# The membrane scan of a spiking mixer: three chains over thirds of the chunks in place of one chain per batch

## What is computed

```python
def step(carry, inputs):
    ...
    inp_t = r_t * wkv
    reset = spike_fn(mem - THRESH)
    mem = BETA * mem + inp_t - reset * THRESH
    spk = spike_fn(mem - THRESH)
    return ((sa, sb, mem), spk)
```

## Time and profile before

| | |
|---|---|
| Time, median of 3 runs | 629.06 us (627.97 to 631.52) |
| The profiled execution, whole | 630.46 us |
| Its span, first to last instruction | 628.6 us |
| Busy: PE, DVE, ACT, POOL | 81%, 72%, 55%, 49% of the span |
| Granted PE clock, mean | 0.916 of full speed |
| Instructions of the scan | 256 on DVE, 51.22 to 96.4 us |

### The profile page before, as it was taken

The page is one execution under the profiler, slowest core; times in us unless marked ns, Lnnn a source line. Parts: engine busy times, 40 slices in busy tenths (PEclk is TensorE's granted clock), DMA queues, the critical chain, the costliest instruction groups (busy, mean ns, idle before and its releaser), DMA issues. The chain is left out here.

```text
span 628.6 us, 11742 instructions
## 1 busy us (share of the span) xinstructions
PE 506.1 (81%) x3926; PEld 313.4 (50%) x3926; DVE 454.5 (72%) x1201; ACT 348.9 (55%) x992; POOL 308.4 (49%) x248
## 2 busy tenths in 40 slices
PE   3740004679999999799879999999799887999996
PEld 3310002337677766544336777676444333666774
DVE  4899997688888883645688888883545675257775
ACT  3950000569998996634469999995633332632331
POOL 5660001488888888447578888883100254020000
PEclk9975556699999999899989999999999988799998
DMA  8200000201111112000011111111000000000001
GB/s 296 103 0 1 0 0 2 68 17 44 36 35 36 35 35 83 3 1 1 19 54 38 37 35 35 35 41 31 0 1 1 1 0 0 2 0 1 18 19 33
DMA packets 14048, 18.80 MB, mean 30 GB/s; under 512 B 2171, under 2 KB 8613, under 8 KB 13861
## 3 DMA queue, kind: packets, MB, share of 16 engines
q1 hardware_dynamic: 13700, 17.97, 10.4%
q10 hardware_dynamic: 288, 0.08, 0.1%
HBM read 8.87 MB, written 1.05 MB: 16 GB/s over the span
## 5 line engine op out<-in xcount | busy, mean ns | idle before, releaser
L465 ACT ACTIVATE prob<-psS,nmx 128x128 f32<-128x128 f32 x256 | 89.9, 377 | 22.1 <-DVE nmx L1007 22.1
L583 POOL TENSOR_TENSOR rst<-mv,half 128x4 f32<-128x4 f32 x24 | 24.9, 1036 | 153.0 <-DVE mv L802 137.5
L722 POOL TENSOR_TENSOR rn<-ssq,half 128x16 f32<-128x16 f32 x32 | 93.2, 2913 | 7.0 <-DVE ssq L993 6.6
L714 POOL TENSOR_TENSOR ra<-ra,rb 128x512 f32<-128x512 f32 x64 | 80.2, 1275 | 2.9 <-DVE rb L975 2.9
L352 ACT ACTIVATE lnx<-psT,nmr,rst 128x128 f32<-128x128 f32 x52 | 19.5, 458 | 91.2 <-POOL nmr L584 91.2
L1284 PE MATMUL psQK<-wqkv,hsA 128*128 128x512 f32 x128 | 64.6, 630 | 3.3 <-ACT z L358 2.2
L972 DVE TENSOR_TENSOR ra<-psQK,rope 128x512 f32<-128x512 f32 x64 | 43.9, 685 | 20.4 <-PE psQK L1284 20.3
L1007 DVE TENSOR_REDUCE nmx<-psS 128x4 f32<-128x512 f32 x64 | 41.2, 685 | 21.3 <-PE psS L1363 18.3
L465 ACT ACTIVATION_READ_ACCUMULATOR prob<-psS,nmx 128x1 f32 x256 | 55.5, 217 | 0.0
L730 POOL TENSOR_TENSOR qkn<-ra,rn 128x512 f32<-128x512 f32 x32 | 33.4, 1043 | 35.7 <-DVE qkn L1001 35.7
L1290 PE MATMUL psO<-masks,identb 128*128 128x512 bf16 x12 | 5.3, 630 | 54.8 <-DVE vAB L878 54.8
(11 more groups left out here) (225 smaller groups left out, 1196.5 us busy)
## 6 DMA issues: line engine op xcount, KB each, us to landing
vAB<-vAB SPq DMA_DIRECT2D x62, 128.0 KB, 2.2
wqkv<-in_wqkv SPq DMA_DIRECT2D x2, 768.0 KB, 7.9
big<-in_x SPq DMA_DIRECT2D x4, 256.0 KB, 4.3
ropeb<-in_rope SPq DMA_DIRECT2D x1, 1024.0 KB, 7.3
big<-in_ew SPq DMA_DIRECT2D x2, 512.0 KB, 4.2
out<-big SPq DMA_DIRECT2D x4, 256.0 KB, 2.3
wmod<-in_wmod SPq DMA_DIRECT2D x1, 768.0 KB, 6.4
w<-in_w SPq DMA_DIRECT2D x2, 341.0 KB
```

The source lines that it names most:

```text
L465: act.activation(prob[:, k, :], psS[:, hb, c * P:(c + 1) * P], ACT.Exp, bias=nmx[:, k:k + 1], accum_out=sums[:, n % 2, k:k + 1]).then_inc( ...
L714: pool.tensor_tensor(o, o, rb[:, r], ALU.add).then_inc(s["sum_" + name], 1)
L722: pool.tensor_tensor(rn[:, :], ssq[:, :], half[:, :], ALU.pow).then_inc(s["rn_ready"], 1)
```

## The change

The chunks' range is cut into three parts, 21, 21 and 22 chunks, and a chain takes one such part of both batches: 42, 42 and 44 elements per instruction. A third semaphore, `dve_c`, is added. A step is then six instructions on DVE, three times L874 and three times L878. vst is cleared for two of the three chains by a memset each. The first three passes are written out in a Python loop in place of the device's loop, and the fallback has three chains as well. What a chunk starts from is unchanged: its predecessor's end of the pass before. PE's wait for `dve_b` has the same value and means the same place in the passes.

```diff
--- before.py
+++ after.py
@@ -182,7 +182,7 @@
             ln_t1 ln_var ln_rstd ln_norm ln_t2 ln_out
             xT_fill xT_evac
             kv_mm num_ready ek_ready gek_ready ekv_ready sb_ready den_ready r_mm r_ready rcp_ready quot_ready cur_ready x_mixed
-            dve dve_b act_own pool_own fallback fallback_b rope_ready tabs_phase tabs_ready z_ready hsA_ready
+            dve dve_b dve_c act_own pool_own fallback fallback_b fallback_c rope_ready tabs_phase tabs_ready z_ready hsA_ready
             k_mm q_mm sq_k sq_q ssq_k ssq_q rope_k rope_q sum_k sum_q ssq_max rn_ready q_ready k_ready
             v_fill v_evac qT_fill qT_evac kT_fill kT_evac pT_fill pT_evac oT_fill oT_evac
             s_done negmax p_ready pv_done va_up0 va_up1 va_low0 va_low1 o_norm
@@ -864,19 +864,22 @@
                 return ph[:, :, j:j + SEQ * (NCH - 1) + 1:SEQ]
 
 
-            both = [own, Steps(dve, s["dve_b"])]
-            both[1].did(dve.memset(vst[:, 1, :], 0.0))
+            thirds = [slice(k * NCH // 3, (k + 1) * NCH // 3) for k in range(3)]
+            chains = [own, Steps(dve, s["dve_b"]), Steps(dve, s["dve_c"])]
+            for k in range(1, 3):
+                chains[k].did(dve.memset(vst[:, :, thirds[k]], 0.0))
 
             def membrane_pass(steps):
                 for j in range(SEQ):
-                    for b in range(B):
-                        steps[b].sync()
-                        steps[b].did(dve.scalar_tensor_tensor(out=vst[:, b, :], in0=at(j)[:, b, :], scalar=-0.3,
-                                                              in1=cur[:, b, :, j], op0=ALU.mult, op1=ALU.add))
-                    for b in range(B):
-                        steps[b].sync()
-                        steps[b].did(dve.scalar_tensor_tensor(out=at(j + 1)[:, b, :], in0=at(j)[:, b, :], scalar=-1.0,
-                                                              in1=vst[:, b, :], op0=ALU.is_lt, op1=ALU.subtract))
+                    for k in range(3):
+                        steps[k].sync()
+                        steps[k].did(dve.scalar_tensor_tensor(out=vst[:, :, thirds[k]], in0=at(j)[:, :, thirds[k]], scalar=-0.3,
+                                                              in1=cur[:, :, thirds[k], j], op0=ALU.mult, op1=ALU.add))
+                    for k in range(3):
+                        steps[k].sync()
+                        steps[k].did(dve.scalar_tensor_tensor(out=at(j + 1)[:, :, thirds[k]], in0=at(j)[:, :, thirds[k]],
+                                                              scalar=-1.0, in1=vst[:, :, thirds[k]], op0=ALU.is_lt,
+                                                              op1=ALU.subtract))
 
 
             dve.wait_ge(s["rcp_ready"], NG)
@@ -885,12 +888,9 @@
             dve.wait_ge(s["r_ready"], NG)
             own.one(dve.tensor_tensor(ekv[:, c], ekv[:, c], rsg[:, c], ALU.mult))
             dve.wait_ge(s["cur_ready"], NG - 1)
-            with dve.Fori(0, PASSES - 1) as k:
-                for st in both:
-                    st.enter(k, 2 * SEQ)
-                membrane_pass(both)
-            for st in both:
-                st.leave(PASSES - 1)
+            for _ in range(PASSES - 1):
+                membrane_pass(chains)
+            for st in chains:
                 st.sync()
 
             def checked_pass(steps):
@@ -911,13 +911,13 @@
                 one(dve.tensor_copy(cnti[0:1, 0:1], cntf[0:1, 4:5]))
                 return dve.value_load(cnti[0:1, 0:1], min_val=0, max_val=P * B * NCH)
 
-            changed = checked_pass(both)
+            changed = checked_pass(chains)
             with dve.If(changed != 0):
 
 
-                again = [Steps(dve, s["fallback"]), Steps(dve, s["fallback_b"])]
-                for b in range(B):
-                    again[b].did(dve.memset(vst[:, b, :], 0.0))
+                again = [Steps(dve, s["fallback"]), Steps(dve, s["fallback_b"]), Steps(dve, s["fallback_c"])]
+                for k in range(3):
+                    again[k].did(dve.memset(vst[:, :, thirds[k]], 0.0))
                 changed = checked_pass(again)
                 with dve.If(changed != 0):
                     with dve.Fori(0, NCH) as k:
```

## The result

| | before | after |
|---|---|---|
| Time, median | 628.51 us (4 runs, 627.79 to 631.52) | 638.18 us (4 runs, 635.77 to 641.28) |
| Ratio | | 1.0123 (95%: 1.0088 to 1.0157) |
| Ratio, measured a second time | | 1.0100 (1.0075 to 1.0124) |
| Span of the profiled execution | 628.6 us | 634.6 us |
| Scan, first L874 to L904 | 45.3 us | 52.6 us |

By these ratios the change makes the kernel 1.0 to 1.2% slower, 6.3 to 7.7 us. They are not the quotients of the medians, which lie further apart: 9.7 us here and 7.3 us (638.01 against 630.75) the second time. The four executions of the kernel after differ by 5.5 us among themselves, so the firmest figure for the change is the length of the scan in the trace, +7.3 us. The forecast was +6.5 us with 635.6 us in all, and a range of 632.3 to 641.3. In the changed kernel L876 and L880 are what L874 and L878 were.

What follows compares the result with a forecast made beforehand. The prediction took the membrane scan, uncovered by other engines and running at DVE's own pace, as the bound. +7.1 - 0.76 + 0.15 = +6.5 us on 629.06 gave 635.6 us, range 632.3 to 641.3.

Steps and rivals of the forecast that it cites:

- What sets the pace: Membrane scan: DVE's own pace, 171 ns per instruction, sets it; two chains leave 52 ns slack per phase, no stall to fill.
- Length less 83 ns: Scan on DVE: each instruction starts about 83 ns before its predecessor ends, so pace is its length less 83 ns.
- Step (a): Scan: three instructions per phase instead of two, 397 ns against 341 over 128 phases, +7.1 us; bounds +4.6 and +13.4.
- Step (b): Scan's device loop removed: entry 0.19 us and two pass turns of 0.31 and 0.26 us saved, -0.76 us.
- Step (c): One more memset, and one more wait in the two places where all chains are collected; +0.15 us.
- Step (e): DVE's jump over the skipped fallback after the count: taken as 0, with -3.8 to +3.8 us kept for the range.
- Step (d): PE after the scan: pause before transposes grows from 4.6 to about 5.1 us; clock shift taken as 0, 1.7 us either side.
- The stride's cost as a start-up price: Rival on the scan: the stride's extra cost is fixed per instruction and doesn't shrink with elements; 641.9 us, chance 0.15.
- The waiting chains: Rival on the scan: chains wait for their own previous results, so a third chain makes it faster; 623.3 us, chance 0.04.
- the wash: Rival on the scan: pace purely proportional to elements, so a phase stays 341 ns; 628.4 us, chance 0.07.
- The pace of contiguous rows: Rival on the scan: stride costs nothing, 66 ns at 6 elements plus 1.04 per further element; 624.7 us, chance 0.03.

Runs made afterwards that it cites:

- experiment 4: Kernel before with one chain of all 128 elements instead of two of 64, passes written out; 636.43 us against 630.34, ratio 1.0102.
- two_written: Kernel before with its two chains of 64 kept and only the first three passes written out; 626.11 us against 630.34, ratio 0.993.
- experiment 8: The kernel after measured and profiled once more, unedited; 638.01 us against 630.75 for the kernel before, ratio 1.0100.
- experiment 3: Kernel before with each of its two chains taking half the chunks of both batches, as two rows of 32; 630.92 us against 630.34, ratio 1.0011.
- experiments 5: As the kernel after, but with four chains of 32 elements and a fallback with one chain; 643.27 us in a single execution.
- experiment 7: Against the kernel before: states and currents stored contiguously, passes written out, one-chain fallback; two chains 620.13 us against 629.98, three chains 627.33 us.
- before_near: Kernel before with only the skipped fallback shortened to one chain; 628.77 us against 630.75, ratio 0.9950.

## Why the prediction was right

- *What sets the pace.* Right. Two chains run at DVE's own pace; experiment 4 shows the other state and gives the dependence 34 ns after the end, as the earlier trace rows had it. The argument that decided it, the second instruction of a phase that waits for nothing in that phase, holds.
- *"Length less 83 ns".* As a rule it was wrong, and that it led to nearly the right number is partly luck. Between two executions the same instructions last 253 or 276 ns (before, two_written) at the same 171 ns from start to start, so in two_written the rule would have been "length less 105"; two executions of the kernel after have 220 and 212 ns (experiment 8). The pace belongs to the instruction, the length reported for it also holds something that varies. It would have been sounder to forecast the pace from paces: 171 at 64 elements and 66 at 6 give 1.81 per element, and with it the same 132 ns at 42.7.
- *Step (a), +7.1 us.* The mis-sized term. The pace at 42.7 elements is 134.8 ns, not 132.3, and the slope is 1.70, not 1.8. The rows taken for it were of other operations (L823 with 4 elements, L904 a two-operand comparison); that this is the reason isn't shown. Measured +8.1 us, 52.6 against the 44.5 of two_written. Both bounds, +4.6 and +13.4, held it. The rows of 21 cost nothing, as taken (experiment 3).
- *Step (b), -0.76 us.* In the scan it is -0.78 (two_written) and -0.68 with three chains, but this agreement is partly luck. The forecast counted 0.19 us for the entry. The entry gives back 0.09: the first instruction comes 0.14 us after its releaser with the passes written out, not 0.04, and it lies ahead of the scan as measured. In its place stands the hole of 0.18 us in pass 1, which the prediction put at nothing when it read pass 4 alone. Together the loop's end brings about -0.87 us.
- *Step (c), +0.15 us.* L900 comes 0.13 us after its last result where it was 0.10, L904 likewise: +0.06. The two memsets together take the 0.07 us that one took.
- *Step (e), 0.* The jump is the same, 3.82 us idle in both. That its price can change with the target's place was right, with 2.25 us, not 3.8; it just didn't happen between these two kernels. In two_written it did, and in a forecast for that one the same step would have missed half of the gain.
- *Step (d).* PE's pause before L936's result is 5.7 us, forecast 5.1. From PE's start to L904 it is 0.66 us longer (101.0 to 104.34, before 93.8 to 96.51), and the 12 warming matmuls took 0.42 us less (4.86 for 5.28), which the step didn't have. Executions of one kernel differ by 3 to 4 us beside a different clock, about the whole width of the 1.7 us allowed to each side. The second measurement shows no lasting share of it in the change.
- *The sum.* +6.5 forecast, +7.3 in the scan of the trace (+8.1 for (a), -0.8 for (b)), 6.3 and 7.7 by the two ratios. The first median lay 2.6 us above the forecast: 0.8 is the scan, mostly step (a), and the rest goes with the execution. Step (e)'s wide allowance of 3.8 us to each side was never called on.
- *The rivals.* The stride's cost as a start-up price falls with experiments 5 and 7 (the extra cost grows with the elements: with the stride the pace is linear from 32 to 64, and the stride's share is 21.5 ns at 42.7 elements and 36 at 64). The waiting chains fall with 4, which shows the gap behind a dependence as 34 ns and not 87, the wash with 5. The pace of contiguous rows is real, but only for contiguous operands (experiment 7): the Trainium skill's section on the TRN2 errata in "VectorE: DVE Perf Modes" gives 58 cycles (60 ns) and one per element, and the runs show 69 ns and 1.04 there; with the stride they show 63 ns and 1.70. The penalty for each access to a new 16-byte line that "SBUF — State Buffer" names, section "Door 1: The DMA port swizzle", agrees with the runs in kind: contiguous rows are cheaper, the more so the more elements. Its size, 0.65 ns per element, comes from them alone, and which of the strided operands pays it wasn't tried.

## What to carry to other kernels

Another independent chain helps only where an engine stands idle between the links of those it has. Before adding one, compare the time from start to start with length plus the gap of a true dependence: where it is larger, each further instruction costs its fixed part, here 63 ns, once in each of the 128 phases. Then look at what an element costs: the layout that made the operands contiguous took 9.1 us off the scan, while one, three and four chains all made it longer than two. And where a forecast is met, check its parts: twice here (step (b), and the time of one chain) a sum came out right over two errors that cancelled.

## What the hardware showed unexpectedly

- The length that the profile gives for a DVE instruction isn't its share of the engine. For the same instructions it was 253, 260 and 276 ns in three executions (before, halves_loop, two_written), at 171 ns from start to start in each, and 220 and 212 ns in two executions of one unchanged kernel at 135 ns.
- A jump on DVE over a part that isn't executed cost 0.6 or 2.9 us, and 2.2 us came or went with edits that touched nothing that runs (before_near). Where a small change moves a time by more than its own instructions can, such a jump is a suspect.
- Operands with a stride of 16 fp32 elements cost 0.65 ns per element more in this operation, 1.70 against 1.04; the fixed part is nearly the same (63 and 69 ns). Together that is 36 ns of 171 at 64 elements.
- An instruction that waits for the one just before it starts 34 ns after that one's end (one_written), while one whose own wait is already over starts 82 ns before it (before: 253 ns long, 171 apart).
